# A Mamba and mixture-of-experts layer on one core: expert tile stages pushed a unit later, output projection at 28 and 30, and a buffer of its own for the residual

## The reference, cut to what matters

```
xn  = layernorm(x)                          # x: 2 x 4096 x 256
out = x + mamba(xn) + experts(xn)           # mamba adds its own residual xn

mamba:   r = rmsnorm(xn) * norm_w ; (xs, z) = r @ in_proj.T       # 256 -> 2 x 512
         u = silu(causal_conv4(xs)) ; (dt, B, C) = u @ x_proj.T
         delta = softplus(dt @ dt_proj.T + b)
         h_t = exp(delta_t * A) * h_(t-1) + (delta_t * u_t) * B_t ; y_t = sum_s h_t[s] * C_t[s]
         return ((y + u * D) * silu(z)) @ out_proj.T + xn         # 16 states, 512 channels

experts: top 2 of 8 per token ; (silu(xn @ w1[e].T) * (xn @ w3[e].T)) @ w2[e].T, weighted, summed
```

## Time and profile before

| what | value |
|---|---|
| median of 3 runs | 2666.92 us (2663.79 to 2672.06) |
| the profiled execution, its own time | 2653.93 us |
| its span, first to last instruction | 2652.2 us |
| mean granted clock of TensorE | 0.936 of full speed |
| busy: DVE, PE, POOL, ACT | 93%, 86%, 77%, 63% |
| issues for x: `xraw<-in_x_dram` | 64 of 256 KB, 2.7 us from issue to landing |

### The profile page before, as it was taken

One profiled execution on the slowest core, in us unless ns is written; L12 is line 12 of the kernel. 1 busy time (PEld: TensorE's weight loads), 2 busy tenths in 40 slices (PEclk: granted clock), 3 DMA queues, 4 the chain that ended last, 5 costly groups with the idle time before them and its releaser, 6 DMA issues. The chain is left out here.

```text
span 2652.2 us, 47132 instructions
## 1 busy us (share of the span) xinstructions
PE 2292.8 (86%) x14442; PEld 1986.7 (75%) x14442; DVE 2459.2 (93%) x4041; ACT 1658.9 (63%) x4137; POOL 2031.0 (77%) x1607
## 2 busy tenths in 40 slices
PE   3958789899999999998999989999989899998665
PEld 2855578878787887877888877888877787887554
DVE  7679999999999999999999999999999999999997
ACT  3940566666666666666666666666666666666653
POOL 3430678888888888888888888888888888888883
PEclk7858899999999999999999999999999999999776
DMA  7216045565555555555555555555555555542451
GB/s 244 92 40 216 29 124 156 154 176 152 161 151 152 157 160 171 158 157 153 155 160 155 166 163 151 158 156 160 154 162 164 156 152 157 159 113 52 96 100 32
DMA packets 267099, 379.38 MB, mean 143 GB/s; under 512 B 21492, under 2 KB 158324, under 8 KB 266852
## 3 DMA queue, kind: packets, MB, share of 16 engines
q1 hardware_dynamic: 236196, 332.26, 40.2%
q0 software_dynamic: 28480, 43.94, 10.1%
q10 hardware_dynamic: 2176, 0.18, 0.1%
HBM read 332.59 MB, written 52.10 MB: 145 GB/s over the span
## 5 line engine op out<-in xcount | busy, mean ns | idle before, releaser
L475 POOL TENSOR_TENSOR h<-du,bbc 128x512 f32<-128x512 f32 x1024 | 1362.5, 1354 | 505.3 <-PE HT L1305 375.3
L1071 DVE TENSOR_TENSOR_SCAN h<-DA,carry,h 128x256 f32<-128x256 f32 x2048 | 1417.7, 734 | 91.4 <-ACT DA L748 79.0
L748 ACT ACTIVATE DA<-delta,alog 128x256 f32<-128x256 f32 x2048 | 882.6, 468 | 212.2 <-DVE h L1071 200.9
L1305 PE MATMUL HT<-ident,h 128*128 128x128 f32 x4096 | 665.8, 288 | 260.5 <-DVE yT L1082 259.1
L1305 PEld LDWEIGHTS HT<-ident,h 128*128 128x128 f32 x4096 | 496.6, 148 | 416.2 <-issue 375.2
L1082 DVE SCALAR_TENSOR_TENSOR yT<-HT,cT,yT 128x512 f32<-128x512 f32 x960 | 698.5, 728 | 3.1 <-PE HT L1305 3.1
L1354 PE MATMUL G<-xtT,W 128*128 128x128 f32 x2160 | 273.2, 281 | 0.0
L1368 PE MATMUL G<-W,fill 128*128 128x256 f32 x1080 | 271.8, 397 | 0.0
L1361 PE MATMUL G<-xtT,W 128*128 128x128 f32 x2160 | 263.4, 275 | 0.0
L1354 PEld LDWEIGHTS G<-xtT,W 128*128 128x128 f32 x2160 | 261.1, 198 | 0.0
L1361 PEld LDWEIGHTS G<-xtT,W 128*128 128x128 f32 x2160 | 252.2, 192 | 0.0
(11 more groups left out here) (183 smaller groups left out, 2986.6 us busy)
## 6 DMA issues: line engine op xcount, KB each, us to landing
W<-in_w_T_dram SPq DMA_DIRECT2D x405, 512.0 KB, 4.2
bbc<-b_dram SPq DMA_DIRECT2D x256, 256.0 KB, 4.3
xraw<-in_x_dram SPq DMA_DIRECT2D x64, 256.0 KB, 2.7
xn_dram<-W SPq DMA_DIRECT2D x8, 1032.0 KB, 14.0
W<-in_x_dram SPq DMA_DIRECT2D x32, 256.0 KB, 6.7
moe_dram<-fill SPq DMA_DIRECT2D x32, 256.0 KB, 4.0
out_dram<-tmpA SPq DMA_DIRECT2D x32, 256.0 KB, 2.2
out_dram<-moe_dram POOLq DMA_DIRECT2D x32, 256.0 KB, 4.4
```

Of the source, the lines that this page charges most:

```text
L475: pool.tensor_tensor(h[:, v % RING], du[:, b, 2 * q:2 * q + 2, :], bbc[:, s // 2 % BRING, s % 2, :].unsqueeze(1).to_broadcast([P, 2, T]), ...
L748: i = act.activation(DA[:, v % 2, k, :], delta[:, b, c, :], ACT.Exp, scale=nega[:, c, s:s + 1])
L1071: i = dve.tensor_tensor_scan(h[:, v % RING, k, :], DA[:, v % 2, k, :], h[:, v % RING, k, :], carry[:, b, s, c:c + 1], ALU.mult, ALU.add)
L1305: i = pe.transpose(HT[:, k, c * P:(c + 1) * P], h[:, (2 * s + c // 2) % RING, c % 2, k * P:(k + 1) * P], ident[:, :])
```

## The change

The third and the first tile of a block get numbers of their own for the steps behind H1: MULT, Y and YO stand a unit later for both, H3 too for the third. The fourth tile starts at 24 instead of 23. The scatter of every tile stands one unit later. `out0` and `out1` move from units 27 and 29 to 28 and 30, `xs1` from 10 to 9, the normalisation from 6 to 2. x for the residual goes to `xres`, a half of a scratch area that is free by then, so that its load waits for the last `result` and not for a normalisation, and `load_x` waits for the last normalisation and stands in unit 3 instead of 31.

```diff
--- before.py
+++ after.py
@@ -150,6 +150,7 @@
         spare = sb("spare", [P, 1])
 
         zs = sb("zs", [P, CH, T])
+        xres = scratch[2][:, 512:1024].rearrange("p (t d) -> p t d", t=NT)
 
         DA = psum("DA", [P, 2, 2, T])
         HT = psum("HT", [P, NT, DI])
@@ -238,7 +239,8 @@
         def tile_of(j, b, v, stage):
 
             for k in range(PER):
-                at = U * (k // len(XT_UNITS)) + XT_UNITS[k % len(XT_UNITS)] + stage
+                at = U * (k // len(XT_UNITS)) + XT_UNITS[k % len(XT_UNITS)]
+                at += stage[k % len(XT_UNITS)] if isinstance(stage, tuple) else stage
                 for pair in (0, 1, -1):
                     if at - 2 * U * pair == U * b + v:
                         return j - pair, k
@@ -267,13 +269,13 @@
             return at // 2 if at >= 0 and at % 2 == 0 and at // 2 < 2 * JB - 2 else None
 
         SLOTS = {"z0": 31, "tanh_z0": 0, "silu_z0": 1, "z1": 2, "tanh_z1": 3, "silu_z1": 4,
-                 "first0": 3, "first1": 4, "y0": 4, "gate_y0": 6, "y1": 5, "gate_y1": 7, "out0": 27, "out1": 29,
+                 "first0": 3, "first1": 4, "y0": 4, "gate_y0": 6, "y1": 5, "gate_y1": 7, "out0": 28, "out1": 30,
                  "oacc": 17, "result": 31,
-                 "normalise": 6, "transpose": 7, "copy_xT": 8, "xs0": 8, "copy_xs0": 9, "xs1": 10, "copy_xs1": 12,
+                 "normalise": 2, "reload": 6, "transpose": 7, "copy_xT": 8, "xs0": 8, "copy_xs0": 9, "xs1": 9, "copy_xs1": 12,
                  "conv0": 11, "conv1": 12, "conv2": 13, "conv3": 14, "tanh_u0": 13, "silu_u0": 14, "tanh_u1": 15, "silu_u1": 16,
                  "x_proj": 17, "copy_xdbc": 18, "dt": 19, "abs": 20, "exp": 22, "ln": 23, "sp0": 24, "sp1": 25,
                  "wm": 23, "corr": 24, "delta": 26, "du": 27, "cT": 25, "copy_cT": 26}
-        XT_UNITS = (4, 13, 18, 23, 30)
+        XT_UNITS = (4, 13, 18, 24, 30)
 
         LOGITS, ROUTE = 2, 3
 
@@ -284,7 +286,8 @@
             return isinstance(j, int) and number(j, b) == 1
 
         INDEX, GATHER = -5, -4
-        XT, XT_COPY, H1, H3, TANH, A2, MULT, Y, YO, SCATTER = 0, 1, 2, 3, 3, 4, 4, 5, 6, 8
+        XT, XT_COPY, H1, TANH, A2, SCATTER = 0, 1, 2, 3, 4, 9
+        H3, MULT, Y, YO = (3, 3, 4, 3, 3), (5, 4, 5, 4, 4), (6, 5, 6, 5, 5), (7, 6, 7, 6, 6)
         W1_LOAD, W3_LOAD, W2_LOAD = 4, 5, 7
 
         def due(name, v):
@@ -299,21 +302,18 @@
             def load_x(j, b):
                 n = number(j, b)
                 sp.wait_ge(s_inT, 16)
-                if isinstance(n, int) and n < 3:
-                    wait(sp, s_xn, 2 * n)
+                sp.wait_ge(s_xn, 2 * n)
+                sp.dma_start(xraw[:, :, :], x_v[b, j]).then_inc(s_x, 16)
+
+            def reload_x(j, b):
+
+                n = number(j, b)
+                sp.wait_ge(s_inT, 16)
+                if n == 0:
+                    sp.wait_ge(s_idx, 1)
                 else:
-                    sp.wait_ge(s_res, n - 2)
-                sp.dma_start(xraw[:, :, :], x_v[b, j]).then_inc(s_x, 16)
-
-            def reload_x(j, b):
-
-                n = number(j, b)
-                sp.wait_ge(s_inT, 16)
-                if isinstance(n, int) and n + 2 >= 2 * JB:
                     sp.wait_ge(s_res, n)
-                else:
-                    sp.wait_ge(s_xn, 2 * (n + 2) + 2)
-                sp.dma_start(xraw[:, :, :], x_v[b, j]).then_inc(s_xres, 16)
+                sp.dma_start(xres, x_v[b, j]).then_inc(s_xres, 16)
 
             def store_b(j, b):
                 n = number(j, b)
@@ -394,11 +394,11 @@
                         load_b(*nxt, v // 4 + LEAD - 8)
                     if unit(j, b, v) < TILES // ZROWS:
                         clear(unit(j, b, v))
-                    if due("normalise", v - 1) and prv:
+                    if due("reload", v) and prv:
                         reload_x(*prv)
                     if due("result", v) and prv:
                         store_out(*prv)
-                    if due("result", v) and nxt and after(*nxt):
+                    if due("normalise", v - 1) and nxt and after(*nxt):
                         load_x(*after(*nxt))
                     if due("copy_xdbc", v - 1) and nxt:
                         store_b(*nxt)
@@ -607,7 +607,7 @@
                 act.wait_ge(s_xres, 16 * (n + 1))
                 for t in range(NT):
                     q = NT * n + t
-                    act.activation(xraw[:, t, :], xraw[:, t, :], ACT.Identity, bias=at_col(nm, q),
+                    act.activation(xres[:, t, :], xres[:, t, :], ACT.Identity, bias=at_col(nm, q),
                                    scale=at_col(onep, q)).then_inc(s_oacc, 1)
 
             def evacuate_rT(j, b):
@@ -1105,7 +1105,7 @@
                 wait(dve, s_mamba, 16 * n)
                 if not isinstance(n, int) or n + 2 < 2 * JB:
                     dve.wait_ge(s_delta, n + 3)
-                dve.tensor_tensor(res, FA[:, :, :], xraw[:, :, :], ALU.add).then_inc(s_res, 1)
+                dve.tensor_tensor(res, FA[:, :, :], xres, ALU.add).then_inc(s_res, 1)
 
 
             stats(0)
```

More of the change, by code:

```diff
@@ L311, in reload_x @@
                 sp.wait_ge(s_inT, 16)
-                if isinstance(n, int) and n + 2 >= 2 * JB:
+                if n == 0:
+                    sp.wait_ge(s_idx, 1)
+                else:
                     sp.wait_ge(s_res, n)
-                else:
-                    sp.wait_ge(s_xn, 2 * (n + 2) + 2)
-                sp.dma_start(xraw[:, :, :], x_v[b, j]).then_inc(s_xres, 16)
+                sp.dma_start(xres, x_v[b, j]).then_inc(s_xres, 16)
             def store_b(j, b):
```

## The result

The changed kernel takes 2682.92 us (median of 5 runs, 2681.12 to 2687.51), the kernel before 2664.99 us (5 runs, 2663.79 to 2672.06): a ratio of 1.0069, 95% interval [1.0046, 1.0092]. It is slower by 18 us. The profiled execution took 2682.85 us (span 2681.1 us, mean granted clock 0.937). It stands at its kernel's median, while that of before lies 11 us under its own, so the two traces differ by 28.9 us and the medians by 18.

The account below looks back on a forecast made before the run. DVE, busy 93% of the span, was taken as the bound. Short blocks +6.7 us, long ones -7.2, blocks without tiles 4: +3.5 on the profiled 2653.9, so 2657; 13 us from profile to median gives 2670; range 2649 to 2686.

Parts of the forecast that it names:

- the clock rival: PE rests once more ahead of the fourth tile's H1, so the clock falls more: 2680 or 2700 us; 3 in 10.
- my own sign: Forecast is wrong if the fourth tile's H1 runs at the low clock in more than four blocks.
- Units 0 to 17: First part of a block: waits of DVE and PE in units 8 and 9 go, 0.8 us gained a block.
- Units 18 to 24: Middle of a block: DVE's saving in unit 22 is waited longer for DA in unit 25; 0, at best 0.25 us.
- Units 25 to 31: End of a block: result waits about 1.1 us for out1, POOL 1.0 to 1.3 us late beside it; 1.15 us lost.
- x, its loads and the normalisation: Normalisation's 1.09 us on ACT hides in unit 3's idle time; new buffer and loads cost nothing.
- The long blocks: Eight blocks with the fourth tile's H1 at low clock: PE's rest shrinks, clock is up again, end part 0.1 us less.
- The tail: Blocks 1 and 29 to 31, without tiles: out1 in unit 30 costs 0.6 us each, more at a low clock; 4 us.

Follow-up runs that it names:

- first_tile_only: The kernel before with only the first tile's MULT, Y and YO a unit later and xs1 in unit 9: 2643.03 us against 2661.88, ratio 0.9928.
- out_back: The changed kernel with out0 and out1 back in units 27 and 29: 2661.75 us against 2661.88 for the kernel before, ratio 0.9995.
- out_scatter_back: The changed kernel with out0 and out1 back at 27 and 29 and the scatter back at 8: 2663.03 us against 2663.19 for the kernel before, ratio 0.9999.
- x_only: The kernel before with only the normalisation in unit 2, the residual's x in its own buffer and the changed loads: 2656.89 us against 2661.02, ratio 0.9987.
- fill_rest: The changed kernel with the transposes of unit 23's state issued three times, ahead of the fourth tile's H1: 2662.67 us against 2661.88 for the kernel before, ratio 0.9993.
- before_fill: The kernel before with the transposes of units 20 and 22 issued three times, in PE's two rests: 2646.14 us against 2663.19, ratio 0.9938.

## Why the prediction was right in its range and wrong in one step

I forecast 2670 us and no change; it is 2683, slower by 0.7%. The stated range of 2649 to 2686 us holds it, but only because the clock rival had been let into the range; the forecast's own, 2660 to 2677, doesn't. By my own sign, more than four blocks with H1 at the low clock, I was wrong: there are 15. On the traces, where I had +3.5 us, it is +28.9; the median of before, 11 us above its profile, hides some of that.

**Units 0 to 17** (0.8 us gained): right. 0.73 measured (42.95 to 42.22 us in nearly every block), and first_tile_only shows that the first tile and `xs1` make it.

**Units 18 to 24** (nothing): right, 17.30 before and after. But the waits moved otherwise than forecast. I had the scan of unit 25 wait longer for DA; instead MULT of the third tile waits longer for H3, 0.66 us where it was 0.25, and the scan no longer waits (in block 13 its DA ends at 1252.62 us and it starts at 1252.66, so ACT's chain has nothing to spare):

```profile
1170.78 0.69 DVE L1047 TENSOR_TENSOR fill<-fill,G 128x512 f32<-128x512 f32 x1 [0.66 <-PE G L1361]
```

That is also why DVE's wait in L1047 fell from 34.4 to 30.3 us only, where I had said 13 less or more: the first tile's 0.5 us went, the third tile's 0.4 came.

**Units 25 to 31** (1.15 lost): right in both mechanisms. 1.03 measured in the short block. The wait of `result`, forecast at 1.07, in block 13:

```profile
1269.61 0.69 DVE L1108 TENSOR_TENSOR tmpA<-FA,W 128x512 f32<-128x512 f32 x1 [1.04 <-PE FA L1378]
```

(x for the residual is shown under the name `W` of its scratch area.) POOL's lateness is not in the changed kernel's waits, as the other covers it; out_back uncovers it, and out_scatter_back removes it. It is 0.9 us (17.42 us from unit 25 on in a short block of out_back, 16.53 before), a little under the 1.0 to 1.3 of the forecast.

**x, its loads and the normalisation** (nothing): right; the interval of x_only, 0.997 to 1.0004, holds 1.

**The long blocks** ("I take it that the clock is then up again when H1 runs"): this step failed. My count was right: PE's rest before H1 is 1.66 us where it was 1.96. The inference from it, that a rest shorter by 0.3 us lets H1 run at the full clock, was not. By the forecast the 8 long blocks' excess would have gone, 10 us won; it grew by 14.5. That is the whole of the error, 24.5 of 25.4 us; the tail (7.2 instead of 4) and the short block (7.8 instead of 9.5) nearly cancel. I made two mistakes. I looked only at the rest right ahead of H1. H1 now has rests of 1.73, 2.38 and 1.66 us before it; before it had 2.25 and 1.96, or 2.25 and 0.40 behind a slow Y. A rest of 1.66 instead of 1.96 us did next to nothing (15 of 22 blocks against 8 of 11); what changed is how often Y was slow and took the full rest away, 5 blocks instead of 16. Why Y is slow less often is open. fill_rest settles that PE's rest is a cause, since it fills the last of the three and H1's low clock is gone; what the first two weigh wasn't tried. And I read block 12 as undisturbed, although the window of its middle part shows a clock of 0.96: the clock fell there too, on a step that costs nothing. The Trainium skill has the rule that I weighed (TensorE: Matmul & The Clock Gate, What's actually happening), that the throttled state is the default and activity releases it. By that rule alone a second rest speaks for more low stretches; the runs agree as to H1, but not in the number of stretches, which fell from 24 to 20. What the rule doesn't give, and the price hangs on, is which step one falls on.

The rival "the clock falls more" named this outcome, 2680 us if H1 runs slow in 8 blocks and 2700 if in all; I gave it 3 in 10. That 2683 lies so near 2680 is luck. There are 15 such blocks, not 8, and each costs 1.6 us, not 1.2, which is 24 us on the forecast's trace of 2657: 2681. I then added 13 us for the distance from profile to median, and the changed kernel's profile has none.

**The tail** (4 us): 7.2. Two windows of the changed kernel, blocks 29 and 30, show a low clock throughout:

```profile
2438.40:2513.20 74.80, 56.70 (x296) 45.36 (x295) 67.90 (x106) 44.12 (x108) 56.69 (x44) 0.82 0.29 61
2513.20:2588.28 75.08, 53.41 (x256) 41.74 (x255) 66.93 (x105) 43.30 (x105) 63.32 (x54) 0.80 0.50 92
```

They took 72.03 and 71.20 us before, at 0.86 and 0.83. The term was of the right kind ("more at a low clock") and too small. It isn't taken apart: out_back's tail is 237.5 us, but out_scatter_back's 241.3.

**Still open** is which blocks turn long. Blocks 12 and 13 have equal rests and part at the third. In the changed kernel long blocks come in rows of 3 to 5, short ones in rows of 3. So a block's length seems to matter through where the next one falls, which would be why out_back and out_scatter_back, alike in the order of PE's units 23 to 27, have 9 and 12; no run tests this alone.

## What to carry to other kernels

Where a kernel runs in a long period and an engine rests in some units, look at the granted clock and at the durations of the same matmul in many periods, not at one: a low stretch on a step that nobody waits for costs nothing, and a reordering can move it onto one that somebody does. A step moved out of a unit leaves a rest there; price the rest as well as the step. If PE rests ahead of a step on the critical path, try filling the rest with matmuls that are thrown away: a loop around four transposes gave 17 us in the kernel before, 20 in the changed one, and with the first tile's part of the change 34 us together.

## What the hardware showed that I had not expected

Adding matmuls can make the kernel faster: before_fill runs 512 more (14954 against 14442), PE's busy share rises from 86% to 88%, and it takes 17 us less. The granted clock, 0.955 to 0.957 in its five runs against 0.933 to 0.941 in the 17 beside it, is what is bought. The Trainium skill says that the penalty of the clock's rise is under 1% of a typical kernel's span, and advises not to fit to a specific count of matmuls at the low clock (TensorE: Matmul & The Clock Gate, What's actually happening). What it describes is the rise once PE is at work. Here the clock falls and rises again in 20 to 24 of 27 blocks; the sum of that agrees in size, 17 of 2663 us being 0.6%, but where changes of 0.3% decide, it is what separated two orders of the same work. And 17 runs of one program, the kernel before, spread over 21 us, those at the lower granted clock being the longer ones, and the first profile lay 11 to 13 us under its median: a single profile can lie 10 us beside it.
